# A convolution and attention kernel on one core: keys and values ahead of a wait, one transform moved by four places, the loop written out

## What is computed

```python
x = x + _L0_conv_ref(_gn(x), g_pos, g_neg, bias, input_factor, output_factor)
x = x + _L1_conv_ref(_gn(x), Wq, Wk, Wv, B, Wm)
```

```python
v = jnp.round(jnp.clip(x, -1, 1) * levels) / levels * VMAX
fv = patches + CUBIC * patches ** 3
outs = [jnp.einsum('bctfyx,ocyx->btfo', fv, g[i]) for i in range(3)]
mem_out = adc(outs[2]) + adc(outs[0]) * 4 + adc(outs[1]) * 2 + adc(outs[2])
result = mem_out * output_factor + bias
```

```python
q, k, v = Wq @ x, Wk @ x, Wv @ x;  ek = jnp.exp(k)
out = Wm @ (q * ((exp(B) @ (ek * v)) / (exp(B) @ ek)))
```

## Time and profile before

| | |
|---|---|
| median of 3 runs | 1491.62 us (1490.83 to 1491.65) |
| the profiled execution | 1491.14 us, span 1489.4 us |
| PE busy | 1426.8 us (96%), 8584 matmuls |
| DVE busy | 1352.5 us (91%) |
| ACT busy | 1201.9 us (81%) |
| POOL busy | 600.1 us (40%) |
| PE's granted clock, mean | 0.99; of the page's 40 slices the second and the last have 8 tenths, all others 9 or more |
| DMA | 103.97 MB, 70 GB/s in the mean |

### The profile page before, as it was taken

How to read it: one execution, slowest core, us unless ns; L and a number is a source line. 1 busy time by engine, 2 the same in 40 slices (tenths; PEclk the granted TensorE clock), 3 DMA queues, 4 the chain that set the end, 5 groups by cost and what they waited for, 6 DMA issues and landing times. The chain is left out here.

```text
span 1489.4 us, 24951 instructions
## 1 busy us (share of the span) xinstructions
PE 1426.8 (96%) x8584; PEld 662.0 (44%) x8584; DVE 1352.5 (91%) x2007; ACT 1201.9 (81%) x1576; POOL 600.1 (40%) x705
## 2 busy tenths in 40 slices
PE   3799999999999999999999999999999999999995
PEld 2444444444444444444444444444444444444442
DVE  6789898999999999998999998899999989999786
ACT  6758788888888888887888978788898888876674
POOL 3612335343433534344353433534243353434323
PEclk9899999999999999999999999999999999999998
DMA  5012012223213222311313231231322222222133
GB/s 213 1 57 57 1 29 57 86 57 113 56 48 96 57 86 57 114 43 52 105 43 99 58 114 32 57 98 52 107 58 71 72 57 86 57 58 57 29 79 121
DMA packets 29187, 103.97 MB, mean 70 GB/s; under 512 B 4032, under 2 KB 4224, under 8 KB 29056
## 3 DMA queue, kind: packets, MB, share of 16 engines
q1 hardware_dynamic: 19984, 70.85, 12.9%
q0 software_dynamic: 8640, 31.46, 11.2%
q10 hardware_dynamic: 432, 0.00, 0.0%
HBM read 37.29 MB, written 33.55 MB: 48 GB/s over the span
## 5 line engine op out<-in xcount | busy, mean ns | idle before, releaser
L552 PE MATMUL A<-T,WH 128*128 128x504 f16 (+1 forms) x1152 | 438.9, 381 | 0.8 <-ACT uall L916 0.5
L553 PE MATMUL A<-T,WH 128*128 128x504 f16 (+1 forms) x1152 | 437.7, 380 | 0.0
L554 PE MATMUL A<-T,WL 128*128 128x504 f16 (+1 forms) x1152 | 437.6, 380 | 0.0
L1692 POOL TENSOR_TENSOR T<-t,T 128x512 f16<-128x512 f32 x192 | 265.9, 1411 | 249.2 <-ACT T L827 249.2
L1668 POOL TENSOR_TENSOR zl<-z,zh 128x512 f16<-128x512 f32 x120 | 155.2, 1310 | 396.2 <-ACT zh L958 396.2
L879 ACT ACTIVATE junk<-xr,shift 128x1024 f16<-128x1024 f32 x244 | 280.1, 1148 | 6.2 <-ACT shift L870 1.0
L552 PE MATMUL B<-T,WH 128*128 128x504 f16 (+1 forms) x576 | 219.7, 381 | 13.3 <-POOL T L1692 11.6
L553 PE MATMUL B<-T,WH 128*128 128x504 f16 (+1 forms) x576 | 219.5, 381 | 0.0
L554 PE MATMUL B<-T,WL 128*128 128x504 f16 (+1 forms) x576 | 219.4, 381 | 0.0
L552 PEld LDWEIGHTS A<-T,WH 128*128 128x128 f16 x1152 | 115.4, 100 | 166.8 <-issue 47.5
L554 PEld LDWEIGHTS A<-T,WL 128*128 128x128 f16 x1152 | 112.8, 98 | 136.5 <-issue 0.6
(11 more groups left out here) (229 smaller groups left out, 2603.7 us busy)
## 6 DMA issues: line engine op xcount, KB each, us to landing
xr<-in_x_dram SPq DMA_DIRECT2D x64, 512.0 KB, 5.9
out_dram<-xr SPq DMA_DIRECT2D x64, 512.0 KB, 2.7
xr<-shared POOLq DMA_DIRECT2D x60, 512.0 KB, 4.6
xr<-in_L_conv_g_pos_dram SPq DMA_DIRECT2D x3, 576.0 KB, 10.7
xr<-in_L_conv_g_neg_dram SPq DMA_DIRECT2D x3, 576.0 KB, 11.4
xr<-in_L_conv_Wm_dram SPq DMA_DIRECT2D x2, 32.0 KB, 10.8
xr<-in_L_conv_Wq_dram SPq DMA_DIRECT2D x1, 32.0 KB, 12.7
xr<-in_L_conv_Wk_dram SPq DMA_DIRECT2D x1, 32.0 KB, 12.4
```

What stands on the lines that cost most here:

```text
L552: nc.tensor.matmul(to, wh, th, start=fresh and y == 1, stop=False, skip_group_check=True)
L553: nc.tensor.matmul(to, wh, tl, start=False, stop=False, skip_group_check=True)
L554: done = nc.tensor.matmul(to, wl, th, start=False, stop=y == 2, skip_group_check=True)
L1692: nc.gpsimd.tensor_tensor(low, t32[:, pair, :, :, :].rearrange("p t e w -> p (t e w)"), high, ALU.subtract).then_inc(tl_ready, 1)
```

## The change

There are three edits.

1. In TensorE's `second_layer`, `keys_values` is called before the waits for the copy of the middle products (`m2_copied`) and for other readers of the low pair, and no longer behind them. `queries` and `mix` stay behind these waits.
2. In `EACH`, for every phase from 1 on: the second group's transform goes from place 29 to 33 on VectorE, its conversion (`HIGH`) from 32 to 34 on ScalarE, its low part (`LOW`) from 33 to 34 on GpSimd, and the fourth group's cubic step from 33 to 29 on VectorE.
3. Phases 2 to 14 are written out in all queues; the hardware loop and its register arithmetic are gone.

```diff
-        "LEVEL": (17, 19, 20, 24), "QUANTISE": (18, 20, 21, 25), "SQUARE": (19, 21, 24, 26), "CUBIC": (20, 22, 27, 33),
-        "TRANSFORM": (26, 29, 3, 11), "HIGH": (30, 32, 6, 14), "LOW": (28, 33, 8, 11)}
+        "LEVEL": (17, 19, 20, 24), "QUANTISE": (18, 20, 21, 25), "SQUARE": (19, 21, 24, 26), "CUBIC": (20, 22, 27, 29),
+        "TRANSFORM": (26, 33, 3, 11), "HIGH": (30, 34, 6, 14), "LOW": (28, 34, 8, 11)}
...
-            for p in range(2, 2 + RING):
+            for p in range(2, B - 1):
                 phase(p, p % RING, (True, True, True, True))
-            with eng.Fori(2 + RING, B - 5, RING) as p:
-                for k in range(RING):
-                    phase(p + k, (2 + k) % RING, (True, True, True, True))
-            phase(B - 2, (B - 2) % RING, (True, True, True, True))
...
+                if values:
+                    keys_values(values[0], values[2], 0)
                 if values or mixed:
...
                 if values:
-                    keys_values(values[0], values[2], 0)
                     queries()
```

## The result

The changed kernel takes 1481.24 us in the median of four runs (1480.43 to 1481.42), the kernel before 1491.61: a ratio of 0.9931, with a 95% interval from 0.9919 to 0.9943. The gain is 10.4 us, the forecast was 12.1. The profiled execution took 1481.24 us, with a span of 1479.2. The page has fewer instructions and a shorter span.

A forecast was written before the change was run, and what follows sets the result against it. TensorE was taken as the bound, with only holes on its row to gain. The terms 2.92 + 2.94 + 7.28 + 0.62 − 1.68 = 12.08 us gave a forecast median of 1479.5 us, range 1477.0 to 1485.5.

The forecast's parts named there:

- TensorE bounds, and holes are the gain: TensorE is busy nearly all of 87.71 us an image; what falls out of its row falls out of the time.
- The written-out loop: Phases 6 to 13: the loop costs 2.92 us, 2.10 in the interval with the jump back; all of it goes.
- Keys and values: Place 32: started ahead of the wait for ScalarE's copy, they save 0.21 us in each of 14 phases, 2.94 us.
- The transform: Place 33: moved four places later on VectorE, it closes the 0.52 us hole after the mix, 14 times, 7.28 us.
- The longer stay of phase 1: From place 32 of phase 1 to phase 5, four images took 0.62 us more than four steady intervals; taken as gone.
- The new wait: Product 1 of the next image waits 0.12 us for ScalarE's rounding of the fifth plane, 1.68 us in 14 images.
- M: Start of the mix (L699) on TensorE at place 33, from which the prediction counted later times in us.
- GpSimd's subtraction is no wait: Second group: starts at M + 3.98, pair ready by M + 5.1 or 5.5, before product 2 at M + 5.84.
- A: Rival: no new wait at product 1, so 1.68 us more gain, 1477.8 us; chance 0.12.
- B: Rival: ScalarE's rounding makes product 1 wait 0.5 us, not 0.12, giving back 5.3 us, 1484.8 us; chance 0.17.
- C: Rival: late phases are slow for another reason, so the loop's 2.92 us stay; with B as well, 1487.7 us; chance 0.05.
- D: Rival: instruction supply in long straight code costs 2.10 us in each of eight formerly looped phases, 1499.2 us; chance 0.04.

The follow-up runs named there:

- the move alone: Kernel before with the second group's transform moved and the loop written out, keys and values still behind the wait: 1483.54 us, ratio 0.9947.
- the loop alone: Kernel before with only the third edit, all phases written out: 1489.81 us against 1491.87, ratio 0.9985.
- the looped phases: Phases 6 to 13 in the changed kernel with the third edit undone, hardware loop put back: 1482.29 us, ratio 0.9934.

## Why the prediction was right, step by step

- **TensorE bounds, and holes are the gain**: right. All intervals are accounted for by distances on its row. Between phases 1 and 14 they sum to 1132.91 us against 1143.68, 10.77 less; 13 intervals of the forecast 87.10 would have been 11.38 less.
- **The written-out loop, 2.92 us**: right for the kernel before (2.81 in the intervals, 2.1 in the medians), but it does not add to the rest. With the holes closed the loop is worth 1.67 us in the intervals and about 1 in the medians.
- **Keys and values, 2.94 us**: the step "they can start 0.31 us after the last product, so 0.21 us goes" failed as a statement about this edit alone, where it gave nothing. As the last of three edits it has the size that was worked out: 87.36 to 87.15. (The view of waits counts this hole 9 times; by distances it stands in all 14 phases.)
- **The transform, 7.28 us**: the hole closed as forecast, at the stated times. It was worth a little more than 0.52 us: behind the old hole the matmuls needed 4.93 us from the sums to product 2, behind the closed one 4.88, so the price of 0.52 was 0.05 too low. Net of the new wait, the move alone brought 0.35 us an image.
- **The longer stay of phase 1, 0.62 us**: right, and it belongs to the move. The interval from phase 1 to 2 was 88.33 us, still 88.33 with the loop alone, and 87.35 with the move.
- **The new wait**: right in place and cause, and mis-sized: 0.19 us and not 0.12. The 8.82 us from L677 to product 1 had in them the 0.05 us by which the matmuls were slower behind the old hole, so TensorE asks at M + 9.68 and not 9.73; and the rounding came 0.02 later than worked out. The 0.05 was missing from the price of the hole as well, and there the two cancel, by luck: product 1 starts when the rounding ends, at M + 9.87 for the 9.85 worked out. The intervals missed by 87.15 − 87.10 = 0.05 us, 0.6 us in 13: 0.02 of it is the later rounding, 0.01 a slower restart of the matmuls behind the new hole, and the rest lies in the rounding of the terms. One experiment in which ScalarE reached the rounding later moved the wait to 0.43, and two in which it did so earlier moved it to zero.
- **GpSimd's subtraction is no wait**: right. It starts at M + 3.98, takes 1.13 us, and product 2 starts at M + 5.79 without a hole.
- **Rivals**: A did not come true. B's larger wait did not come either: the eviction starts 1.16 us behind the mix, as at place 24, and the wait is 0.07 us above the forecast, not 0.38. Its link, that a later eviction costs TensorE time, shows in the looped phases: 0.08 us later, and 0.08 us more of wait. C and D fell with the loop alone.
- **The rest of the 1.7 us** between forecast and median can be placed only in the profiles, whose spans differ by 10.2 us. Of the 1.9 us that are missing there, 0.6 are in the intervals. In the head, place 32 of phase 1 comes 0.24 us later, where the forecast had it 0.21 earlier. From place 32 of phase 14 to the last keys 0.21 us are gained, in both profiles of the changed kernel, where the forecast had 0.52 − 0.12 = 0.40. The end is 0.54 longer in the first profile of the changed kernel, and not in the second. The prediction took head and end as unchanged and gave no reason.

## What to carry to other kernels

Holes on the engine that bounds are worth their length only if the next wait is not for something that keeps its own time: for each hole closed, find what releases the next one, and whether it moves along. Of a task moved behind another engine's result, count the whole queue from that result to the next thing that is waited for; here 8.65 us of ScalarE's work, from the eviction's start to the end of the rounding, had to fit into the 8.52 from M + 1.16 to M + 9.68, and with 0.06 us until TensorE goes on that makes the wait of 0.19. In this kernel, filling the queue's idle time, with GpSimd's work kept away from VectorE's clippings, brought the interval from 87.15 to 86.95 us; taking work out of the queue, with GpSimd's part of it beside those clippings, brought it to 87.22.

## What the runs showed of the hardware

- The one jump back of a hardware loop cost VectorE 3.99 us of standing still in one kernel and 2.52 us in the other with the same loop, and TensorE 2.1 and 1.1 us in the interval. With all phases written out, the late intervals were as short as the early ones (87.14 or 87.15 us).
- Clippings of 128 × 2048 int16 on VectorE took 0.68 and 0.69 us alone, and 1.28 and 1.65 beside two subtractions of GpSimd with float32 input, which themselves took 2.73 us instead of 2.27. The mixing of products (one operand in PSUM) ran beside GpSimd without a loss on either side: its row L1295 takes 0.70 us with and without GpSimd at work, and three subtractions take 3.39. Beside the cubic step, with both operands in SBUF, three took 4.47.
- A matmul started 0.06 us behind the end of the ScalarE instruction that released it, and 0.15 behind VectorE's.
